# A ring of one-hot groups, two count accumulators and shared banks in the first sort of a graph kernel

## What is computed

```python
edge_index = jnp.stack([src, dst])
h = jnp.maximum(_layernorm(x), 0.0)
x = x + _L0_gnn_ref(h, edge_index, edge_attr_8, ...)   # softmax attention over the edges of each dst
h = jnp.maximum(_layernorm(x), 0.0)
x = x + _L1_gnn_ref(h, edge_index, ...)                # two more layers, segments by src
```

## Time and profile before

| | us |
|---|---|
| median of 3 runs | 4108.05 (4103.3 to 4112.84) |
| the profiled execution | 4080.52 |
| its span in the profile | 4078.7 |
| busy in the span: TensorE / VectorE / ScalarE / GpSimd | 2017.6 / 1638.2 / 892.8 / 2104.0 |

### The profile page before, as it was taken

The page is one execution under the profiler, slowest core; times in us unless marked ns, Lnnn a source line. Parts: engine busy times, 40 slices in busy tenths (PEclk is TensorE's granted clock), DMA queues, the critical chain, the costliest instruction groups (busy, mean ns, idle before and its releaser), DMA issues.

```text
span 4078.7 us, 42134 instructions
## 1 busy us (share of the span) xinstructions
PE 2017.6 (49%) x10220; PEld 1740.9 (43%) x10220; DVE 1638.2 (40%) x5782; ACT 892.8 (22%) x2543; POOL 2104.0 (52%) x2168
## 2 busy tenths in 40 slices
PE   1165454555434333320201984666666746666666
PEld 0043333333323333320201873665666636666665
DVE  6186655445412222233201552333333533333336
ACT  0013333333210000000000112333333323333332
POOL 4514444444456666667775004555556255555651
PEclk9999999999955555555555556666666766666666
DMA  2000000000022222220000003333333333333331
GB/s 63 1 1 3 3 3 3 3 3 3 3 81 72 69 70 67 69 40 1 1 1 1 1 1 110 95 101 101 97 100 101 63 103 101 102 97 99 102 101 30
DMA packets 127587, 211.06 MB, mean 52 GB/s; under 512 B 59466, under 2 KB 70412, under 8 KB 126988
## 3 DMA queue, kind: packets, MB, share of 16 engines
q0 software_dynamic: 82944, 146.87, 13.4%
q1 hardware_dynamic: 44428, 61.51, 5.4%
HBM read 193.75 MB, written 14.47 MB: 51 GB/s over the span
## 4 chain that ended last, share of the span: by engine, by line
another core or an unknown queue 39%; PE 26%; DVE 19%; issue 10%; ACT 4%; DVEq 1%; DMA 1%; POOL 0%; ACTq 0%; SPq 0%; POOLq 0%
PE PS L1249 6%; PE PS L1026 5%; PE PS L1259 4%; PE PS L881 3%; DVE arena L386 2%; PE PS L534 2%; DVE work L1177 2%; DVE red L1182 1%; PE PS L1261 1%; ACT arena L556 1%; PE PS L489 1%; PE PS L507 1%; DVE work L1169 1%; DVE work L1194 1%
## 5 line engine op out<-in xcount | busy, mean ns | idle before, releaser
L589 POOL DMA_INDIRECT sorted_d<-S,rows x416 | 401.8, 966 | 556.0 <-DVE rows L466 429.1
L1157 POOL DMA_INDIRECT arena<-kv_d,S x528 | 514.5, 974 | 336.9 <-DVE work L1194 188.3
L1157 POOL DMA_INDIRECT kv<-kv_d,S x352 | 343.6, 976 | 590.8 <-DMA S<-grouped_d 279.5
L1249 PE MATMUL PS<-arena,work 128*128 x1760 | 385.9, 387 | 476.5 <-DVE work L1177 408.2
L1249 PEld LDWEIGHTS PS<-arena,work 128*128 128x128 f32 x1760 | 333.7, 282 | 499.1 <-issue 499.0
L1259 PE MATMUL PS<-work,R 128*128 128x128 f32 x1760 | 524.4, 392 | 35.9 <-issue 32.3
L801 POOL DMA_INDIRECT kv<-kv_d,S x440 | 417.3, 948 | 240.1 <-issue 128.2
L598 POOL DMA_INDIRECT grouped_d<-pay,rows x416 | 419.9, 1009 | 170.1 <-issue 131.9
L1216 ACT ACTIVATE R<-iota,gate 128x128 f32<-128x128 f32 x880 | 279.8, 388 | 742.0 <-remote 653.8
L881 PE MATMUL PS<-R,work 128*128 x880 | 238.2, 430 | 396.4 <-issue 317.7
L1261 PEld LDWEIGHTS PS<-wts,R 128*128 128x128 f32 x1760 | 374.5, 261 | 55.6 <-issue 55.0
(11 more groups left out here) (253 smaller groups left out, 2946.5 us busy)
## 6 DMA issues: line engine op xcount, KB each, us to landing
work<-segT_d SPq DMA_DIRECT2D x165, 256.0 KB
kv<-kv_d,S POOLq DMA_INDIRECT x792
arena<-kv_d,S POOLq DMA_INDIRECT x528
grouped_d<-pay,rows POOLq DMA_INDIRECT x416
sorted_d<-S,rows POOLq DMA_INDIRECT x416
kv_d<-arena SPq DMA_DIRECT2D x12, 512.0 KB, 2.9
sorted_d<-S SPq DMA_DIRECT2D x1, 2200.0 KB, 7.7
S<-sorted_d SPq DMA_DIRECT2D x1, 2200.0 KB, 8.8
```

Source lines behind the costliest of these rows:

```text
L589: gp.indirect_dma_start(out=sorted_d, out_offset=bass.IndirectOffsetOnAxis(ap=rows0[0:n, c:c + 1], axis=0), in_=S0[0:n, c, :], in_offset=N ...
L1157: gp.indirect_dma_start(out=ring[s][:, j, :], out_offset=None, in_=kv1_d[l], in_offset=bass.IndirectOffsetOnAxis(ap=S1[:, t, 1:2], axis=0) ...
L1249: done = nc.tensor.matmul(banks[7][:, j * DM:(j + 1) * DM], RT[:, g % 2, j * P:(j + 1) * P], table[:, ds(blocks[g % 3][j] * (3 * DM), DM)] ...
```

## The change

- The one-hot buffers become a ring of `ONES` = 16 groups. In stage 1 TensorE signals once per `AHEAD` = 4 groups, and VectorE waits only every fourth group, for the signal of the groups that used the same slots 16 groups ago. In stage 2 VectorE makes the one-hots two groups ahead rather than one.
- Two accumulators `H[0]` and `H[1]` (banks 0 and 5): pair u is read from `H[u % 2]`. To go from pair u to pair u+2 an accumulator needs two pairs' counts, so TensorE does four count products per pair and not two. ScalarE copies into a ring of four Hs.
- Keys and lookups of a pair share one bank, and there are `TABLES` = 3 such banks. The signal `s_bc` is gone; VectorE waits on `s_look` for both.
- The transposed one-hots have three buffers and are made two groups ahead; the diagonals have 16 columns and are made two groups ahead.

```diff
@@ sort_vector
             for g in range(NEG):
-                since(dve, s_ohu, g - 1)
-                onehots(g, g % 2)
+                if g % AHEAD == 0:
+                    since(dve, s_ohu, (g - ONES) // AHEAD + 1)
+                onehots(g, g % ONES)
...
             for g in range(NEG):
-                b, q, s = g % 2, g // QUAD, g % QUAD
-                if g + 1 < NEG:
-                    dve.wait_ge(s_h, g * (EG // 2) + 1)
-                    since(dve, s_first, g * EG)
-                    onehots(g + 1, 1 - b)
+                b, q, s = g % ONES, g // QUAD, g % QUAD
+                if g + 2 < NEG:
+                    since(dve, s_look, (g + 3 - ONES) * (EG // 2))
+                    since(dve, s_first, (g + 3 - ONES) * EG)
+                    onehots(g + 2, (g + 2) % ONES)
                 for j in range(EG):
...
-                    dve.wait_ge(s_bc, u + 1)
+                    dve.wait_ge(s_look, u + 1)
                     nc.vector.scalar_tensor_tensor(
...
-                    dve.wait_ge(s_look, u + 1)
@@ sort_tensor
+            def count_pair(n, u):
+                c = 2 * u
+                count(n, (c // EG) % ONES, c % EG)
+                return count(n, (c // EG) % ONES, c % EG + 1)
             for g in range(NEG):
                 pe.wait_ge(s_oh, g + 1)
                 for j in range(EG):
-                    done = count(g % 2, j)
-                done.then_inc(s_ohu, 1)
+                    done = count(0, g % ONES, j)
+                if g % AHEAD == AHEAD - 1:
+                    done.then_inc(s_ohu, 1)
...
-                    count(b, 2 * k)
-                    count(b, 2 * k + 1).then_inc(s_h, 1)
+                    done = count_pair(u % 2, u)
+                    if u + 1 < EC // 2:
+                        done = count_pair(u % 2, u + 1)
+                    done.then_inc(s_h, 1)
                     pe.wait_ge(s_diag, 2 * u + 2)
-                    since(pe, s_rank, 2 * u - 2)
+                    since(pe, s_rank, 2 * (u - TABLES) + 2)
+                    since(pe, s_first, 2 * (u - TABLES) + 2)
...
-                                     start=True, stop=True).then_inc(s_bc, 1)
-                    since(pe, s_first, 2 * u - 2)
+                                     start=True, stop=True)
@@ sort_scalar
-                    if u + 1 < EC // 2:
-                        since(act, s_look, u)
-                        table(u + 2, (u + 1) % 2)
-                    if g + 1 < NEG:
-                        since(act, s_bc, u - 1)
+                    if u + 2 < EC // 2:
+                        table(u + 2)
+                    if g + 2 < NEG:
+                        since(act, s_look, u - 3)
```

More of the change, by code:

```diff
@@ L28 @@
 NQ = NEG // QUAD
+ONES = 16
+AHEAD = 4
+TABLES = 3
 T = 440
@@ L345, in since @@
                 eng.wait_ge(semaphore, value)
-        H = banks[0][0:HI, 0:P]
-        KEYS = [banks[2 + n][:, 0:2 * P] for n in range(2)]
-        LOOK = [banks[4 + n][:, 0:2 * P] for n in range(2)]
+        H = [banks[n][0:HI, 0:P] for n in (0, 5)]
+        KEYS = [banks[2 + n][:, 0:2 * P] for n in range(TABLES)]
+        LOOK = [banks[2 + n][:, 2 * P:4 * P] for n in range(TABLES)]
         ATP = banks[6].bitcast(f16)[0:HI, 0:EG * P].rearrange("p (j e) -> p j e", j=EG)
@@ L413, in sort_vector @@
             nc.vector.tensor_copy(tiles_f, tiles_i).then_inc(s_tiles, 1)
-            onehots(0, 0)
+            for g in range(2):
+                onehots(g, g)
             dve.wait_ge(s_tiles, 1)
@@ L494, in sort_tensor, with transposes @@
                 for j in range(EG):
-                    done = count(g % 2, j)
-                done.then_inc(s_ohu, 1)
+                    done = count(0, g % ONES, j)
+                if g % AHEAD == AHEAD - 1:
+                    done.then_inc(s_ohu, 1)
             pe.wait_ge(s_seed, 1)
-            nc.tensor.matmul(H, ident[0:HI, 0:HI], seed, start=True, stop=True,
-                             skip_group_check=True).then_inc(s_h, 1)
+            for n in range(2):
+                done = nc.tensor.matmul(H[n], ident[0:HI, 0:HI], seed, start=True, stop=True, skip_group_check=True)
+            done.then_inc(s_h, 1)
             pe.wait_ge(s_tiles, 1)
             nc.tensor.matmul(STARTS, above[0:HI, 0:HI], tiles_f, start=True, stop=True).then_inc(s_starts, 1)
-            def transposes(g, b):
+            def transposes(g):
                 pe.wait_ge(s_oh, NEG + g + 1)
@@ L506, in transposes @@
                 for j in range(EG):
[L507 removed]
+                    done = nc.tensor.transpose(ATP[:, j, :], A16[:, g % ONES, j, :], ident16[:, :])
                 done.then_inc(s_at, 1)
@@ L555, in diagonal, with transposed, table @@
             def diagonal(c):
[L556 removed]
+                nc.scalar.activation(diag[:, c % (4 * EG), :], ident16[:, :], ACT.Copy,
                                      scale=keyc[:, c:c + 1]).then_inc(s_diag, 1)
[L559 removed]
+            def transposed(g):
                 act.wait_ge(s_at, g + 1)
[L561 to L568 removed]
+                nc.scalar.copy(AT16[:, g % 3, :, :], ATP)
+                nc.scalar.copy(AT[:, g % 3, :, :], ATP).then_inc(s_ats, 1)
+            def table(u):
+                act.wait_ge(s_h, u + 1)
+                since(act, s_look, u - 3)
+                nc.scalar.copy(Hs[:, u % 4, :], H[u % 2]).then_inc(s_hs, 1)
+            for c in range(2 * EG):
                 diagonal(c)
[L570 to L571 removed]
+            table(0)
+            transposed(0)
+            table(1)
+            transposed(1)
             for g in range(NEG):
```

71 lines of the change are left out of this document (32 added, 39 removed).

## The result

The changed kernel takes 4117.9 us (median of 20 runs) against 4102.0 (20 runs) on the same chip: ratio 1.004, 95% interval 1.0025 to 1.0055. It is slower, by only 0.4% but with an interval that leaves out 1, where 3909 us and faster was forecast. Measured once more (experiment 5) it came to 4118.8 us (10 runs) against 4102.3 (13), ratio 1.0046 [1.002, 1.0072].

What follows compares the result with a forecast made beforehand. It took the first sort, a chain of waits on TensorE signals delayed while scatters run, as the bound. 4080.5 - 58 (stage 1) - 141 (stage 2) = 3881.5, plus 27.5 to the median: 3909 us, range 3810 to 4000.

Steps and rivals of the forecast that it cites:

- I take the service: one signal after another: Both sort stages: TensorE's signals pass singly, each slower the longer scatters run, one per 11.2 us in stage 1.
- A: The forecast itself, a service per signal: 3909 us, own range 3860 to 3960, chance 0.50.
- B: Plain delay, signals late but passing together: quads of 24 us, 27 with steps, 3848 us in all, chance 0.20.
- Stage 1, -58: Stage 1, to the reading of the counts: fewer signals and 16 groups outstanding gain 58 us.
- floor of 40: Stage 1: the smallest gain allowed, 40 us, with signals 11.2 us apart from the start on.
- Stage 2, -141: Stage 2: fewer signals and more depth bring quads to 26 or 29 us, 680 us against 821.
- Costs that I set at nothing: Mainly stage 2's two added count products per pair, 46 us of TensorE, taken as hidden by its idle half.
- C: Stage 2: less time without scatters leaves late signals, quads settle at 30 us, 3984 us in all, chance 0.20.
- D: Scatters slowed by denser one-hots beside them, 4.2 to 8 us a quad: about 4030 us, chance 0.05.
- E: TensorE's clock falls to 1.2 GHz in the sort, quads of 38 us: 4179 us, slower, chance 0.03.
- F: The waits are not those of TensorE's signals and nothing moves: 4108 us, chance 0.02.
- The distance to the median: Whole kernel: the median of the runs lies 27.5 us above the profiled execution, kept for the changed kernel.

Runs made afterwards that it cites:

- experiment 5: The changed kernel and the kernel before measured again, and the changed one with spaced scatters: ratio to the kernel before 1.0046, and 0.9353 with spaced scatters.
- e1: Kernel before, with TensorE signalling after each of a group's four count products in stage 1: 4083.1 us against 4101.5.
- e2: Kernel before, with two further unused TensorE products a group in stage 1 and the old signals: 4110.7 us.
- e11: Kernel before, with each pair's two one-hot products worked out once more ahead of the lookups: 3019.1 us against 2987.9.
- f6: Changed kernel, with a GpSimd memset after every indirect DMA: 3485.2 us, ratio 0.8521 to the kernel before.
- e3: Kernel before, with only the ring of 16 groups and a signal per four in stage 1: 4078.9 us, ratio 0.9961.
- e5: Kernel before, with a short GpSimd memset after each scatter of stages 1 and 2: 3855.4 us, ratio 0.9334.
- f4: Kernel before, with a GpSimd memset of 128 words per lane after every indirect DMA: 3433.8 us, ratio 0.839.
- e9: All first-sort scatters held back until all rows are worked out: 3487.4 us in the kernel before, 3525.3 in the changed one.
- e4: Changed kernel, with stage 1 of the kernel before: 4122.4 us, ratio 1.0052 to the kernel before.
- f3: Changed kernel, with scatters spaced by 1.46 us: 3829.7 us, ratio 0.9353 to the kernel before.

## Why the prediction was wrong, point by point

- **What bounds the kernel**: right that the first sort, not GpSimd's issue, sets the end, and that waits grow and end with the scatters. The step that failed first is "I take the service: one signal after another". The signals are late, that much was right, but not at a price for each signal: four times the signals left a group at 11.20 us, and four more TensorE instructions a group made it 16.80 (e1, e2). The price is 1.40 us for each instruction of the sender, eight to a group, and for VectorE's own as well. Both my models, service and plain delay, were models of a signal, so A and B, 0.70 of the chance, fell together.
- **Stage 1, -58**: measured -8.5, below my floor of 40. With TensorE's signal off the way, VectorE's own five instructions a group are next, 7.0 us, where I had them at 0.85. When the waits end at 192 us VectorE has begun its 37th group instead of its 27th, and ten groups at 0.85 us are the 8.5 us. TensorE's backlog is not the bound: 30 products run in 3.34 us at 192.07. The floor of 40 took "the same 11.2 us from the start on" for the worst case of a signal and let VectorE's own work run free.
- **Stage 2, -141**: measured +15.7. Fewer signals (29 to 21) count for nothing (e1, in stage 1), and two pairs of depth are used up in a wait of 11.8 us at 886.42.
- **"Costs that I set at nothing"**: the two further products a pair. I named 46 us as their price if TensorE's idle half were not there to hide them. Its idle half was idle by the toll, and where the toll is gone TensorE is the bound (81% busy) and the products cost 31 to 33.5 us by themselves (e11). The rebuilt stage cost +15.7 and +25.4 us with the toll, +34.5 without, +42 with all DMAs spaced (one profile each); the bound of 46 was the better term. Beside the toll the added instructions are not charged 1.40 us each: 32 more a quad would be 45 us, but quads 11 to 25 take 32.2 and 32.1 us, and only the first ten grow, by 1.7. Why those do is not shown.
- **Rivals**: C (cover goes) was not it: the changed kernel's stalls end 22.8 us after the first scatter, and long waits do not stand in the first 6 us of a quad. D did not occur: scatters stayed at 1.26 us in the changed kernel; once they are spaced and the one-hots have no gap, a part of it does (1.19 us for 0.97, 11 us in all in f6). E's event occurred, its price did not: the clock fell to 0.50 and e3's stage 2 took 822.0 us against 821.3. F (nothing moves, 0.02) was nearest with 4108; its reason, that the waits are not those of TensorE's signals, is half right: in the kernel before VectorE does wait for them, but in the changed one it stands in stage 1 without waiting for any.
- **What would show it wrong** was put rightly: "stage 2 stays at 32 us a quad, which would say that neither depth nor the number of signals is what holds it". It stayed at 32.1 in the quads without steps of the second sort and 35.5 in those with them.
- **The distance to the median**: kept at 27.5 us, and 21.5 to the median of 20 runs; the profiled run of the kernel before was among its fastest, that of the changed one lies 6 us above its median. The medians differ by 16 us, the last scatters by 9.8.

**Open**: what the 1.40 us is, and why one chip in four has no toll. Every run on record has a span and a granted clock of the profiler, so none shows whether the toll is there when nothing is recorded. Why e5 took 656 us for stage 2 and f4 600 with the same spacing of 1.46: VectorE's longest wait there is 2.9 us in e5 and 1.9 in f4, and they ran on different chips and wrote the memset to different tiles. A spacing between 1.26 and 1.46 us was not tried.

## What to carry to other kernels

Before you call a wait a slow signal, divide it by the number of instructions that the sender has ahead of the signal, and look whether short instructions that wait for nothing start at equal distances; if they do, the count of instructions is the cost, and depth and fewer signals help little (here 8.5 us of 58 in one stage, a loss in the other). Don't book added work on an engine as hidden because it is idle for half the time: ask what it is idle for, and whether the change is to remove just that. Where indirect DMAs are issued back to back beside other work, try them a little further apart (here 0.2 us, 16% of the kernel), on more than one chip, since where no toll is the spacing only costs: the changed kernel with spaced scatters is 3.2% over the kernel before there, and e9 lets the change itself account for about 35 of these 96 us.

## What the runs showed of the hardware that I had not expected

- Indirect DMAs issued every 1.26 us hold VectorE and TensorE to one instruction per 1.40 us in the long run, on three chips of the four in the experiments (VectorE 7.0 us for 5, TensorE 11.2 for 8 and 16.8 for 12); at 1.46 us the toll is gone or nearly so. TensorE runs ahead of it for a while (eight instructions per 7.0 us until about 130 us), with its signals late, before its products are spaced too. It doesn't depend on the rows: 32 instead of 128 leave it as it is.
- The fourth chip has none at 1.26 us: 2988 us against 4102, the same program. The Trainium skill, "SBUF — State Buffer", section Who interferes with whom, holds that a DMA never contends with a compute engine. These runs don't show contention for a port, but they show compute engines held while indirect DMAs are issued at 1.26 us and free, or nearly, at 1.46.
- TensorE's granted clock fell to 0.50 (1.2 GHz) in stage 2 when the ring was in and the toll too (e3, in most runs), stayed 1.00 without the ring (e4), and stayed 1.00 with the ring when scatters were spaced (f3, f6). At 0.50 the stage took the same 822 us, and a key product and its lookups start 0.32 us apart (869.72 and 870.04) as they do at 1.00 (702.05 and 702.37).
